# Routed expert stage: order of the weight split, Gelu chunks in pairs, four chunks of lead, eight chunk buffers

## The reference

```python
def _experts_mlp(x, g, W1, b1, W2, b2):
    xn = _rmsnorm(x, g)
    h = jnp.einsum('btc,ech->bteh', xn, W1) + b1        # C = 256, H = 1024
    h = jax.nn.gelu(h, approximate=False)
    return jnp.einsum('bteh,ehc->btec', h, W2) + b2

scores = jax.nn.sigmoid(u @ centroids)
gpk, i_topk = jax.lax.top_k(scores, K)                  # K = 2 of 8
gk = gpk / scores.sum(axis=-1, keepdims=True)
routed_all = _experts_mlp(u, g_routed, W1_r, b1_r, W2_r, b2_r)
routed_topk = jnp.take_along_axis(routed_all, i_topk[..., None], axis=2)
h_r = (gk[..., None] * routed_topk).sum(axis=-2)
return u + h_s + h_r
```

## Time and profile before

| | us |
|---|---|
| median of 3 timed runs | 1440.33 |
| lowest, highest | 1437.97, 1440.91 |
| the profiled execution | 1436.01 |
| its span, first to last instruction | 1434.3 |

### The profile page before, as it was taken

One profiled execution on the slowest core, in us unless ns is written; L12 is line 12 of the kernel. 1 busy time (PEld: TensorE's weight loads), 2 busy tenths in 40 slices (PEclk: granted clock), 3 DMA queues, 4 the chain that ended last, 5 costly groups with the idle time before them and its releaser, 6 DMA issues. The chain is left out here.

```text
span 1434.3 us, 22326 instructions
## 1 busy us (share of the span) xinstructions
PE 1170.9 (82%) x7861; PEld 1008.2 (70%) x7861; DVE 1026.1 (72%) x2507; ACT 793.5 (55%) x1454; POOL 389.5 (27%) x397
## 2 busy tenths in 40 slices
PE   0363698797897987997978988599999999999996
PEld 0142477576676666775766777589888999899886
DVE  2356659568567676595684654588898889888984
ACT  2101355444553554554544443488888887888785
POOL 2312122041041121221410201144334433443343
PEclk9986799999999999999999998799999999999998
DMA  4899910000010010000000000677777777777772
GB/s 125 220 265 273 288 61 30 30 30 30 30 59 30 20 41 30 30 31 30 30 15 15 31 19 27 213 206 194 194 218 210 198 190 214 216 198 194 205 220 24
DMA packets 172563, 168.08 MB, mean 117 GB/s; under 512 B 48362, under 2 KB 159860, under 8 KB 172452
## 3 DMA queue, kind: packets, MB, share of 16 engines
q1 hardware_dynamic: 120884, 109.43, 25.3%
q10 hardware_dynamic: 37264, 38.54, 10.5%
q0 software_dynamic: 14304, 18.69, 6.3%
HBM read 109.42 MB, written 57.22 MB: 116 GB/s over the span
## 5 line engine op out<-in xcount | busy, mean ns | idle before, releaser
L1233 DVE TENSOR_TENSOR wlo<-raw,whi 128x512 fp32r<-128x512 f32 x312 | 228.2, 732 | 35.1 <-ACT whi L1184 31.4
L1155 PE MATMUL bank<-xhi,whi 128*128 128x256 f32 x624 | 178.8, 287 | 25.5 <-issue 20.2
L1206 ACT ACTIVATE hraw<-bank,b 128x256 f32<-128x256 f32 x312 | 148.2, 475 | 86.2 <-PE bank L1155 53.1
L1273 DVE TENSOR_TENSOR hlo<-hraw,hhi 128x256 fp32r<-128x256 f32 x312 | 183.1, 587 | 17.5 <-ACT hhi L1209 5.7
L973 PE MATMUL bank<-whs,shared_hhi 128*128 128x256 f32 x512 | 150.0, 293 | 50.1 <-DVE shared_hlo L727 50.1
L1135 PE MATMUL bank<-whi,hhi 128*128 128x256 f32 x624 | 180.3, 289 | 12.8 <-issue 11.4
L523 ACT ACTIVATE shared_hraw<-bank,b1s 128x512 f32<-128x512 f32 x128 | 88.1, 688 | 180.8 <-PE bank L988 171.4
L1155 PE MATMUL bank<-xlo,whi 128*128 128x256 f32 x624 | 175.3, 281 | 0.0
L1155 PE MATMUL bank<-xhi,wlo 128*128 128x256 f32 x624 | 175.1, 281 | 0.0
L1135 PE MATMUL bank<-whi,hlo 128*128 128x256 f32 x624 | 173.4, 278 | 0.0
L1135 PE MATMUL bank<-wlo,hhi 128*128 128x256 f32 x624 | 173.3, 278 | 0.0
(11 more groups left out here) (248 smaller groups left out, 2834.7 us busy)
## 6 DMA issues: line engine op xcount, KB each, us to landing
raw<-in_L_ffn_W_r_dram SPq DMA_DIRECT2D x78, 1024.0 KB, 7.8
sorted_tokens<-base ACTq DMA_DIRECT2D x1, 33540.0 KB, 137.6
xt<-sorted_tokens SPq DMA_DIRECT2D x39, 260.0 KB
big<-in_L_ffn_W_s_dram SPq DMA_DIRECT2D x4, 1024.0 KB
xb<-in_x_dram SPq DMA_DIRECT2D x8, 512.0 KB, 4.6
cb<-in_ctx_dram SPq DMA_DIRECT2D x8, 512.0 KB, 3.6
xr<-in_x_dram SPq DMA_DIRECT2D x8, 512.0 KB, 3.6
out_dram<-base ACTq DMA_DIRECT2D x8, 512.0 KB, 2.9
```

Source lines behind the costliest of these rows:

```text
L1155: last = nc.tensor.matmul(ub[:, 0:T], w[i][:, wsl], x_[i][:, k, :], start=k == 0 and t == 0, stop=k == KD - 1 and t == 2)
L1206: nc.scalar.activation(hraw[:, m % NHB, :], psum[m % NU][:, 0:T], ACT.Gelu, bias=b1[i][:, m:m + 1]).then_inc(t_gelu, 1)
L1233: nc.vector.tensor_tensor(wlo[i][:, psl], raw[i][:, psl], whi[i][:, psl].bitcast(fp32), ALU.subtract).then_inc(t_wlo, 1)
L1273: nc.vector.tensor_tensor(hlo[:, m % NHB, :], hraw[:, m % NHB, :], hhi[:, m % NHB, :].bitcast(fp32), ALU.subtract).then_inc(t_hlo, 1)
```

## The change

Four things are changed, all in the routed stage.

- The second product follows four chunks behind the first (`LAG` = 4), and there are eight chunk buffers (`NHB` = 8).
- The cast and the subtraction of the Gelu's output are made for two chunks at once, in the odd steps: four casts and four subtractions of 512 columns in the place of eight and eight of 256.
- In step m the queues take piece m of the next tile. In tile 0, steps 0 to 3 take its own W2 pieces, and steps 4 to 7 two pieces each of tile 1. On VectorE the piece now comes ahead of `xT` and ahead of the tokens' subtraction; ScalarE and GpSimd wait for the first products of the tile two before for W1 pieces, and for its second products for W2 pieces.
- GpSimd casts `xhi` ahead of the two indirect DMAs, no longer behind them.

```diff
         stage_c = ExitStack()
-        NHB = 4
+        NHB = 8
+        LAG = 4
...
-        def piece_of(m):
-
-            return (m - LAG) % M, m >= LAG
-
         XSTEP = 3
+
+        def pieces_at(n, m):
+            if n == NT - 1:
+                return []
+            if n == 0:
+                return [2 * (m - NP1), 2 * (m - NP1) + 1] if m >= NP1 else []
+            return [m]
...
                 def second(n, i, m):
 
-                    pe.wait_ge(t_hhi, M * n + m + 1)
-                    pe.wait_ge(t_hlo, M * n + m + 1)
                     if m % 2 == 0:
+                        pe.wait_ge(t_hhi, (M * n + m) // 2 + 1)
+                        pe.wait_ge(t_hlo, (M * n + m) // 2 + 1)
                         pe.wait_ge(t_wlo, M * n + NP1 + m // 2 + 1)
...
                     if n > 1 and m == 0:
-
+                        sc.wait_ge(t_up, M * (n - 1))
+                    if n > 1 and m == NP1:
                         sc.wait_ge(t_step, M * (n - 1))
...
-                        sc.wait_ge(t_gelu, M * n + m + 1)
-                        nc.scalar.copy(hhi[:, m % NHB, :], hraw[:, m % NHB, :]).then_inc(t_hhi, 1)
+                        if m % 2:
+                            h = m % NHB
+                            sc.wait_ge(t_gelu, M * n + m + 1)
+                            nc.scalar.copy(hhi[:, h - 1:h + 1, :], hraw[:, h - 1:h + 1, :]).then_inc(t_hhi, 1)
                         if m == LAG and n > 0:
                             output(n - 1, 1 - i, r - 1 + i)
-                        piece, ahead = piece_of(m)
-                        if not ahead:
-                            weights(n, i, r, piece)
-                        elif n < NT - 1:
+                        if n == 0 and m < NP1:
+                            weights(0, 0, 0, NP1 + m)
+                        for piece in pieces_at(n, m):
                             weights(n + 1, 1 - i, r + i, piece)
...
                     for m in range(M):
-                        dve.wait_ge(t_hhi, M * n + m + 1)
-                        nc.vector.tensor_tensor(hlo[:, m % NHB, :], hraw[:, m % NHB, :],
-                                                hhi[:, m % NHB, :].bitcast(fp32), ALU.subtract).then_inc(t_hlo, 1)
-                        piece, ahead = piece_of(m)
-                        if not ahead:
-                            weights(n, i, piece)
-                        elif n < NT - 1:
+                        if m % 2:
+                            h = m % NHB
+                            dve.wait_ge(t_hhi, (M * n + m) // 2 + 1)
+                            nc.vector.tensor_tensor(hlo[:, h - 1:h + 1, :], hraw[:, h - 1:h + 1, :],
+                                                    hhi[:, h - 1:h + 1, :].bitcast(fp32), ALU.subtract).then_inc(t_hlo, 1)
+                        if n == 0 and m < NP1:
+                            weights(0, 0, NP1 + m)
+                        for piece in pieces_at(n, m):
+                            weights(n + 1, 1 - i, piece)
+                        if n < NT - 1:
                             if m == XSTEP:
                                 tokens(n + 1, 1 - i)
                             if m == M - 2:
                                 tokens_low(n + 1, 1 - i)
-                            weights(n + 1, 1 - i, piece)
                             if m == M - 1:
                                 owners(n + 1, 1 - i)
...
                     if n > 1:
-
-                        pool.wait_ge(t_step, M * (n - 1))
+                        pool.wait_ge(t_up if m < NP1 else t_step, M * (n - 1))
...
                     if n < NT - 1:
                         weights(n + 1, 1 - i, r + i, BY_POOL[0])
+                        tokens(n + 1, 1 - i)
                     if n > 0:
                         add_up(n - 1, 1 - i)
                     if n < NT - 1:
-                        tokens(n + 1, 1 - i)
                         weights(n + 1, 1 - i, r + i, BY_POOL[1])
```

More of the change, by code:

```diff
@@ L1197, in body @@
                     if n == 0:
-                        for m in range(M - LAG):
+                        for m in range(NP1):
                             weights(0, 0, 0, m)
```

## The result

| | before, us | changed, us |
|---|---|---|
| median of 6 runs each | 1439.18 | 1427.01 |
| lowest, highest | 1435.84, 1440.91 | 1426.03, 1430.55 |
| profiled execution | 1436.01 | 1426.37 |
| its span | 1434.3 | 1424.5 |
| routed stage, first product to last | 505.9 | 494.4 |

The ratio is 0.9914, with a 95% interval of 0.9901 to 0.9927: 12.2 us less by the medians, where 11.4 less (1428.9) was forecast. Three more rounds in another series gave 0.9923 (0.9892 to 0.9954), 11.7 less.

A forecast was written before the change was run, and what follows sets the result against it. No engine was full in the routed stage; PE stopped twice a tile, waiting for VectorE's hlo and xlo. Terms -14.2 (37 tiles), +1.7 (start), +1.1 (end) gave -11.4 us: 1440.3 to 1428.9, range 1418 to 1447.

The forecast's parts named there:

- The first stop goes: TensorE's 0.37 us idle at a second product, waiting for hlo, is hidden by the longer lead: worth 0.53 us a tile.
- The second stop stays: Stop before a tile's first matmul now waits for xlo behind wlo(6) and ScalarE's chain: 12.61 us a tile, gain 14.2.
- GpSimd: xhi cast comes off the path; later weight casts meet hlo(6,7) and wlo(7) under about 2 us of cover, costed at nothing.
- Loads: W1 and W2 weight loads for the next tile stay hidden, by 3 us at the worst landing.
- Start: Tile 0: VectorE must make all pieces of tile 1 and hlo(4,5) ahead of xlo: +1.7 us (0 to +3).
- the timetable: The prediction's summed times of each engine's operations, counted from a tile's first matmul.
- End: After the last tile's first products, four second products remain instead of two: 14.3 us instead of 13.2, +1.1.
- Sum: Routed stage: -14.2 + 1.7 + 1.1 = -11.4 us, from 1440.3 to 1428.9.
- The slower rival: GpSimd's whi(7) cast gets in ahead of xlo on VectorE, 0.62 us: tile 13.23, 1452 us in all; chance 0.15.
- The much faster rival: ScalarE runs ahead and TensorE works through without a stop: 11.70 us a tile, -45, 1395 us; chance 0.08.
- A row against a rule: Whether a GpSimd cast can hold an already started VectorE subtraction: xlo unheld by the rule, by the row 1.1 us a tile.

## Why the prediction was right, point by point

- **The first stop goes.** Right: no idle time at a second product. With GpSimd's order undone or with single chunks there is none either, so in these kernels the lead of four is enough for it; the pairs aren't needed, and with a lead of two they make four such stops a tile. But GpSimd's new order alone, with a lead of two and single chunks, takes nearly all of this stop away too, which the forecast didn't see.
- **The second stop stays, on up(4), ScalarE, wlo(6), xlo.** Right in each link: from the tile's start at 1147.24, gelu(4) at 7.00 (7.01 forecast), gelu(6) at 10.17 (10.19), whi(6) done at 11.15 (11.19), xlo done at 12.47 (12.50), restart at 12.57 (12.61). The undone link, wlo(6) ahead of xlo, gives back 28 us. The term was 14.2 us and measured 15.2. One comparison in the working is uneven: it set the 0.91 of this stop, a whole loss, beside 0.57 + 0.37, which are idle times alone. With the 0.16 that each stop costs on top, the two were 1.26 before, and the one is now 0.72 + 0.16 = 0.88.
- **GpSimd.** xhi right: 0.62 long, starting 8.53 after the tile's start (8.47). The casts came later than forecast, at 12.73 and not 12.04, since the two indirect DMAs lasted 1.82 and 1.86 instead of 1.54. Why they did isn't settled. The cover for hlo(6,7) held: it ended at 1161.71, and its product came after 1163.
- **Loads.** Right: W2 landed in 9.8 us at most, and no engine waited for one in the steady part.
- **Start.** Mis-sized: +1.7 forecast, +2.6 measured (tile 0 takes 14.48, not 11.89). Up to xT the timetable held: xT ended 8.74 after the tile's start, forecast 926.0 - 917.32 = 8.7. What was too small is the row of subtractions behind it, put at 0.60 each with nothing in the way. GpSimd's casts of xhi and of piece 3 fell into it, and held a wlo and hlo(4,5) by 0.4 each:

```profile
927.50 1.70 DVE L1239 TENSOR_TENSOR wlo<-raw,whi 128x512 fp32r<-128x512 f32 x2
929.12 1.09 DVE L1281 TENSOR_TENSOR hlo<-hraw,hhi 128x512 fp32r<-128x512 f32 x1
```
```profile
927.65 1.01 POOL L1311 CAST xhi<-xT 128x512 fp32r<-128x512 f32 x1 [4.38 <-DVE xT L1248]
928.60 1.07 POOL L1304 CAST whi<-raw 128x512 fp32r<-128x512 f32 x1
```

  That is 0.8 of the missing 0.9. The term's own bounds, 0 to +3 "with GpSimd in the way or not", had named it. TensorE's clock rose later in this tile than before (granted 0.50 from 923 to 924 us, where the kernel before had 1.00 from 921 to 922), but no part of the miss needs it, since xT came on time.
- **End.** +1.1 forecast, 14.4 against 13.2 measured: +1.2.
- **Sum.** 15.2 - 2.6 - 1.2 = 11.4 us less in the stage, the forecast's number, through two errors of 1 us that cancel. In the profiled pair the stage began 1.5 us later (918.84, 917.32), in work that the change doesn't touch; so the spans differ by 9.8. The medians differ by 12.2.
- **The slower rival** didn't happen, and that was in part luck. xlo ran from 11.79 to 12.47 after the tile's start and the cast's row began at 12.73. By my timetable that row would have begun at 12.04, inside xlo's, and in six kernels a subtraction in that place was held (next point). The cast came late only because the two DMAs before it lasted 1.82 and 1.86 instead of the 1.54 of my row, for a reason that no run shows. The rival's price was also too low: I gave it one cast of 0.62, 0.24 us a tile net. In the runs more than one subtraction of the path is held, and behind a stop of over 2.5 us the clock can fall: 4 to 8% slower than the changed kernel. The range's upper end, 1447, was far from what such a case costs.
- **The much faster rival** had the right size: 45 us less without a stop, and 44.0 measured with xlo in step 5. It takes one more edit, xlo one place earlier, which the forecast's own sum pointed to.
- **A row against a rule.** Both have a part. In six kernels a subtraction whose row starts 0.15 to 0.34 us before a cast's was held all the same. In all of them the cast stands behind an indirect DMA, and its row starts before that DMA's ends (1159.97 against 1160.53), so its start is no safe sign of when it took the port. The DMA itself holds nothing: xlo, inside the DMA's row but ahead of the cast's, took its 0.68. Where no DMA stands before the cast, the first does keep its place, as in the kernel with GpSimd's order alone: hlo starts 0.17 before the cast and isn't held, the cast lasts 0.71, and the wlo behind it 1.10:

```profile
1154.96 0.42 DVE L1273 TENSOR_TENSOR hlo<-hraw,hhi 128x256 fp32r<-128x256 f32 x1
1155.29 1.10 DVE L1233 TENSOR_TENSOR wlo<-raw,whi 128x512 fp32r<-128x512 f32 x1
```
```profile
1155.13 0.71 POOL L1297 CAST whi<-raw 128x512 fp32r<-128x512 f32 x1 [1.52 <-PE bank L1135]
```

  The Trainium skill, "SBUF — State Buffer", "Who interferes with whom", lets the first one keep the port and has the other wait for it. These rows agree with it, and so do the ends of the held ones in the changed kernel, which go by turns: the first cast at 1161.16, hlo(6,7) at 1161.71, the second cast at 1162.16, wlo(7) at 1162.72 (GpSimd, then VectorE):

```profile
1159.97 1.19 POOL L1304 CAST whi<-raw 128x512 fp32r<-128x512 f32 x1
```
```profile
1161.64 1.08 DVE L1239 TENSOR_TENSOR wlo<-raw,whi 128x512 fp32r<-128x512 f32 x1
```

  So the 2.08 of hlo(6,7) are the time to the end of a DMA and one cast, not two. Turns aren't kept everywhere: the wlo of 2.45 waited for two casts of three (the third ended 0.46 after it), and the xhi of 1.62 for a run of subtractions. Why isn't settled.

## What to carry to other kernels

When a change takes a wait away, write down what stands last in the queues behind the wait that is left, link by link from rows: here this gave the tile to 0.03 us, and the one instruction to move next. Test the parts of a change alone: one part, xhi ahead of two slow DMAs, was worth three times the whole, because another part put a late weight piece ahead of the operand that the next tile starts with. And look how far a gain is from a collision: with half a microsecond more on ScalarE, or with less work on GpSimd, the changed kernel gets 4 to 8% slower.

## What the runs showed of the hardware that was not expected

- VectorE's subtractions of two operands in SBUF and GpSimd's casts hold each other up, mostly by turns: a subtraction of 512 columns lasted 1.08 to 1.10 instead of 0.68 us behind one cast. Longer holds occurred as well: 2.45 with three casts queued, of which two went first, and a cast of xhi of 1.62 instead of 0.68 with three subtractions queued.
- A cast behind an indirect DMA holds VectorE from before the DMA's row ends: subtractions whose rows began 0.15 to 0.34 us ahead of such a cast's were held in six kernels. One that began 0.17 ahead of a cast without a DMA before it was not.
- A stop of TensorE of 2.6 to 3.1 us a tile was followed in some tiles by the low level of its clock, 1.2 GHz (0.59 and 0.62 granted over 3 and 4.5 us; 0.94 between 1000 and 1350 us); with stops of 2.0 us this happened in four tiles of 37 (0.99), and with stops of 0.7 us in none of the steady part (1.00).
- The indirect DMA's row lasts 1.54 to 1.56 us in some orders and 1.7 to 2.1 in others, for the same work.
- A kernel can settle in one rhythm and leave it: the same instructions took 11.62 us a tile for some ten tiles and 12.57 after.
